# Splitting and shifting the token preparation inside a sixteen-head attention loop

## The reference

```python
def _layer_norm(x, scale, offset):
    mu = jnp.mean(x, axis=-1, keepdims=True)
    var = jnp.var(x, axis=-1, keepdims=True)
    return (x - mu) * jax.lax.rsqrt(var + LN_EPS) * scale + offset
...
h = _layer_norm(x, ln1_scale, ln1_offset)
x = res + _cross_attention(h, xf_1, ...)      # 16 heads: q from h, k and v from the context
h = _layer_norm(x, ln2_scale, ln2_offset)
x = res + _cross_attention(h, xf_2, ...)
h = _layer_norm(x, ln_mlp_scale, ln_mlp_offset)
h = gelu(h @ w_fc1 + b_fc1) @ w_fc2 + b_fc2
return x + h
```

## Time and profile before

| | before |
|---|---|
| median of 3 runs | 1243.47 us (1241.01 to 1245.72) |
| profiled execution: its time | 1242.29 us |
| profiled execution: its span | 1240.8 us |
| busy, PE / DVE / ACT / POOL | 1198.8 / 888.7 / 779.0 / 598.1 us |
| mean granted TensorE clock | 0.995 |

### The profile page before, as it was taken

How to read it: one execution, slowest core, us unless ns; L and a number is a source line. 1 busy time by engine, 2 the same in 40 slices (tenths; PEclk the granted TensorE clock), 3 DMA queues, 4 the chain that set the end, 5 groups by cost and what they waited for, 6 DMA issues and landing times.

```text
span 1240.8 us, 27130 instructions
## 1 busy us (share of the span) xinstructions
PE 1198.8 (97%) x9933; PEld 1027.3 (83%) x9933; DVE 888.7 (72%) x2304; ACT 779.0 (63%) x1889; POOL 598.1 (48%) x966
## 2 busy tenths in 40 slices
PE   9999999999999999999989899999999899999997
PEld 8999999999999999999978565786675587666664
DVE  6887868778887787778864788536788564667764
ACT  5876666668866666566774566746776643555553
POOL 4874645558865454555852443504444131324333
PEclk9999999999999999999999999999999999999999
DMA  6541001104430001001320220122322012221100
GB/s 193 157 123 32 27 26 33 34 27 123 142 94 27 26 28 34 27 27 35 123 70 27 81 81 29 52 73 71 88 64 70 20 54 61 59 65 44 39 11 19
DMA packets 56820, 75.03 MB, mean 60 GB/s; under 512 B 11312, under 2 KB 30576, under 8 KB 56688
## 3 DMA queue, kind: packets, MB, share of 16 engines
q1 hardware_dynamic: 51568, 72.75, 19.5%
q0 software_dynamic: 5120, 0.56, 0.3%
HBM read 49.46 MB, written 1.05 MB: 41 GB/s over the span
## 4 chain that ended last, share of the span: by engine, by line
PE 81%; DVE 7%; issue 5%; ACT 4%; POOL 2%; DMA 1%; ACTq 0%; DVEq 0%; POOLq 0%
PE bank L125 19%; PE bank L127 18%; PE bank L126 18%; PE bank L2053 5%; PE bank L771 4%; PE bank L2000 3%; PE bank L2010 3%; PE bank L1986 2%; PE bank L2011 2%; ACT PT L2127 2%; PE bank L1982 2%; PE bank L178 1%; DMA Q<-rows 1%; PE bank L713 1%; PE bank L1737 1%
## 5 line engine op out<-in xcount | busy, mean ns | idle before, releaser
L1095 POOL TENSOR_SCALAR E<-E,rl 128x256 f32<-128x256 f32 x256 | 243.8, 963 | 213.6 <-DVE rl L980 213.4
L2127 ACT ACTIVATE PT<-bank 128x512 f32<-128x512 f32 x320 | 173.4, 594 | 92.2 <-PE bank L2011 56.0
L846 ACT ACTIVATE QTh<-bank,bqs 128x256 fp32r<-128x256 f32 x128 | 60.7, 474 | 151.4 <-PE bank L127 151.3
L2208 DVE CUSTOM_DVE_ANT_0 Em<-bank,M 128x256 bf16<-128x256 f32 x256 | 95.1, 420 | 53.7 <-PE bank L1986 22.3
L856 ACT ACTIVATE E<-bank,nm 128x257 f32<-128x257 f32 x256 | 119.4, 480 | 1.2 <-DVE nm L950 1.1
L984 DVE TENSOR_TENSOR PTl<-bank,PTh 128x512 fp32r<-128x512 f32 x128 | 88.0, 688 | 27.6 <-ACT PTh L868 27.1
L957 DVE SCALAR_TENSOR_TENSOR QTl<-bank,bqs,QTh 128x256 fp32r<-128x256 f32 x128 | 61.6, 481 | 63.0 <-ACT KT L847 62.2
L868 ACT CAST PTh<-bank 128x512 fp32r<-128x512 f32 x128 | 75.2, 587 | 43.7 <-PE bank L771 43.6
L2202 DVE TENSOR_REDUCE nm<-bank 128x1 f32<-128x512 f32 x128 | 83.4, 686 | 22.1 <-PE bank L1982 21.4
L950 DVE TENSOR_REDUCE nm<-bank 128x1 f32<-128x257 f32 x256 | 95.4, 415 | 0.0
L2000 PE MATMUL bank<-Q,K 51*128 51x256 f32 (+1 forms) x640 | 85.5, 315 | 4.4 <-DMA Q<-rows 1.9
(11 more groups left out here) (438 smaller groups left out, 4374.5 us busy)
## 6 DMA issues: line engine op xcount, KB each, us to landing
stage<-in_wts SPq DMA_DIRECT2D x99, 256.0 KB, 3.3
U<-in_vrows SPq DMA_DIRECT2D x64, 256.0 KB, 2.7
K<-stage SPq DMA_DIRECT2D x48, 128.0 KB
Q<-stage SPq DMA_DIRECT2D x48, 128.0 KB
K<-stage SPq DMA_DIRECT2D x48, 64.0 KB
Q<-stage SPq DMA_DIRECT2D x48, 64.0 KB
K<-xh SPq DMA_DIRECT2D x16, 128.0 KB, 3.0
Q<-rows POOLq DMA_DIRECT2D x96, 4.0 KB, 1.8
```

The lines of the kernel that those rows point to most:

```text
L1095: m = pool.tensor_scalar(s.E[:, i % 3, t, 0:256], s.E[:, i % 3, t, 0:256], s.rl[:, r, t:t + 1], None, ALU.mult)
L2127: act.activation(s.PT[i % s.NPT][:, 2 * u:2 * u + 2, :].rearrange("p a b -> p (a b)"), s.STB[y][:], ACT.Exp).then_inc(S["t_ex"])
L2208: dve.tensor_tensor_reduce(out=s.Em[:, (2 * i + e) % 4], in0=bank[:, e * 256:e * 256 + 256], in1=s.M3[:, j, e, :], scale=-1.0, scalar=3.4e ...
```

## The change

Counted modulo 16, for the seven seams:

| step | engine | pass before | pass after |
|---|---|---|---|
| statistics | VectorE | 7, both tiles and the aggregation | 6 and 7, one tile each; aggregation in 8 |
| root | GpSimd | 7 | 8 |
| normalisation | VectorE | 8, both tiles | 9 and 10, one each |
| `turn_x` | TensorE | 9 | 11 |
| scaling | VectorE | 10, both halves | 12 and 13, one each |
| `tokens_high`, `tokens_low` | ScalarE, VectorE | 11 | 14 |

The first MLP batch's steps move from passes 114, 115, 116, 118 to 111, 112, 113, 114 and 116; the second one's statistics from 119 to 118 and its scaling from 121 to 122. The number of operations and their sizes stay as they are.

```diff
-AHEAD = {114: [(0, "stats")], 115: [(0, "norm")], 116: [(0, "turn"), (0, "scale")], 118: [(0, "parts")],
-         119: [(1, "stats")], 120: [(1, "norm")], 121: [(1, "turn"), (1, "scale")], 127: [(1, "parts")]}
+AHEAD = {111: [(0, "stats")], 112: [(0, "norm")], 113: [(0, "turn")], 114: [(0, "scale")], 116: [(0, "parts")],
+         118: [(1, "stats")], 120: [(1, "norm")], 121: [(1, "turn")], 122: [(1, "scale")], 127: [(1, "parts")]}
...
-        if t % 16 == 9 and t // 16 < 7:
+        if t % 16 == 11 and t // 16 < 7:
             turn_x(t // 16 + 1)
...
-        if t % 16 == 11 and t // 16 < 7:
+        if t % 16 == 14 and t // 16 < 7:
             tokens_high(t // 16 + 1)
...
+    def half_stats(n, t):
+        w.wait_ge(S[f"ld_x{n}"] if n < 4 else S["dve_x"], 16 if n < 4 else n - 3)
+        z = dve.bn_stats(s.scr["st"][:, t, :], batch_x(n)[:, t, :])
...
+    def half_norm(n, t):
+        w.wait_ge(S["dve_hlo"], n)
+        w.wait_ge(S["ln_rsqrt"], n + 1)
...
-            if t % 16 == 7:
-                stats(n)
+            if t % 16 in (6, 7):
+                half_stats(n, t % 16 - 6)
             if t % 16 == 8:
-                norm(n)
-            if t % 16 == 10:
-                scaled(n)
-            if t % 16 == 11:
+                moments(n)
+            if t % 16 in (9, 10):
+                half_norm(n, t % 16 - 9)
+            if t % 16 in (12, 13):
+                half_scaled(n, t % 16 - 12)
+            if t % 16 == 14:
                 tokens_low(n)
...
-            if t % 16 == 7:
+            if t % 16 == 8:
                 rsqrt(t // 16 + 1)
```

More of the change, by code:

```diff
@@ L925, in stats, with moments @@
         ln_stats(dve, w, S, "ln", n, batch_x(n), s.scr)
+    def half_stats(n, t):
+        w.wait_ge(S[f"ld_x{n}"] if n < 4 else S["dve_x"], 16 if n < 4 else n - 3)
+        z = dve.bn_stats(s.scr["st"][:, t, :], batch_x(n)[:, t, :])
+        if t == 1:
+            z.then_inc(S["ln_stats"])
+    def moments(n):
+        w.wait_ge(S["ln_stats"], n + 1)
+        dve.bn_aggr(s.scr["mv"][:, 0, :], s.scr["st"][:, 0, :])
+        dve.bn_aggr(s.scr["mv"][:, 1, :], s.scr["st"][:, 1, :]).then_inc(S["ln_moments"])
+    def half_norm(n, t):
+        w.wait_ge(S["dve_hlo"], n)
+        w.wait_ge(S["ln_rsqrt"], n + 1)
+        z = dve.tensor_scalar(xn[:, t, :], batch_x(n)[:, t, :], s.scr["mv"][:, t, 0:1], s.scr["rs"][:, 4 + t:5 + t],
+                              ALU.subtract, ALU.mult)
+        if t == 1:
+            z.then_inc(S["ln_xn"])
     def norm(n):
@@ L929, in norm, with half_scaled @@
         ln_norm(dve, w, S, "ln", n, batch_x(n), s.scr)
+    def half_scaled(n, d):
+        a = n // 4
+        w.wait_ge(S["pe_hT"], n + 1)
+        w.wait_ge(S["ld_cols"], 16)
+        z = dve.tensor_scalar(xn[:, d, :], s.MISC[:, d * 256:d * 256 + 256], c.col("ln_s", a, d), c.col("ln_o", a, d),
+                              ALU.mult, ALU.add)
+        if d == 1:
+            z.then_inc(S["dve_hf"])
     def scaled(n):
```

## The result

The changed kernel takes 1254.1 us, the median of 6 runs (1250.56 to 1255.09), against 1243.49 for the kernel before: a ratio of 1.0079, 95% interval 1.0067 to 1.0092, thus 8 to 11 us slower. Its profiled execution took 1253.96 us, its span is 1252.5.

What follows compares the result with a forecast made beforehand. TensorE, busy 97% of the span, bounds the kernel. Waits +10.9, port +1.0, gains -4.0 make +7.9 us: 1250.2 from the profiled 1242.29, put at 1250.8 as halfway to the median's offset; range 1246.5 to 1256.

Steps and rivals of the forecast that it cites:

- The sign and its cause: Slower, chance 0.76: in heads 15 modulo 16 TensorE waits for `hTl`, which runs behind `PTl`; sum +7.9 us.
- the port lost everywhere: Rival, chance 0.12: GpSimd wins the shared port at all seven seams, 3.6 us in place of 1.0; about 1253.4.
- the gains absent: Rival, chance 0.08: the removed waits return behind another operation, only 1 us gained; +10.9, about 1254.
- The wait's size: TensorE's wait for `hTl` at each seam: 1.44 us standing still, 1.55 with refill, 10.9 for seven.
- The port: VectorE and GpSimd contend for a port at `hTl`; two of seven seams lost, 2 x 0.52 = 1.0 us.
- The trace agrees on who blocks whom: Claim that the trace fits the skill's first-comer lock rule, though head 41 shows 0.52 us, not the rule's 0.78.
- The clock: Rival, chance 0.03: standing still halves TensorE's clock for a head, another 4.7 us per seam, +33 in all.
- The gains: Waits removed: five seams 1.4, seam 1 0.75, seam 4 0.85, MLP batches 1.0; together 4.0 us.
- the 0.2 that was to come back in heads 58 and 62: Seam 4: heads 56 and 60 lose their waits, 0.2 us returns in heads 58 and 62; net -0.85.
- The MLP's part: First and second MLP batch, heads 112, 116 and 120: moving their steps forward saves 1.0 us.
- hidden by one whole head: GpSimd's root, moved one pass, costs nothing: the normalisation needing it comes two half steps later, covered by 4.72 us.
- The forecast's own range: +5.5 to +10.5 us, chance 0.62, from the port's bounds and gains between 2.5 and 5.4.

Runs made afterwards that it cites:

- e1: The changed kernel with both token steps still in pass 14, but ahead of `heads_out` and `probs` on ScalarE and VectorE: 1241.79 us.
- e2: The kernel before with only the two token steps moved from pass 11 to pass 14, nothing split: 1253.99 us.
- e6: The kernel of e1 with the two token steps back in their late place in pass 14 at the first seam alone: 1243.47 us.
- e8: The changed kernel with two more unread tile statistics on VectorE ahead of each `hTl` of the loop, 0.34 us each: 1257.52 us.
- e4: The changed kernel with GpSimd's root moved from the end of pass 8 to pass 9, behind the key column: 1250.62 us.
- e3: The kernel before with only the new `AHEAD` table for the MLP's first tokens: 1242.86 us, ratio 1.0000.
- e10: The kernel before, nothing split: statistics and root moved to pass 6, token steps to pass 12, plus the MLP's new table: 1239.47 us.

## Why the prediction came out as it did

**The sign and its cause were right.** 1254.1 lies within 1246.5 to 1256, and the mechanism is shown both ways: e1 takes the wait away and leaves the splitting, e2 leaves the splitting out and makes the wait. The number alone would not show this: two of the rivals, at 1253.4 (the port lost everywhere) and 1254 (the gains absent), lie nearer to 1254.1 than the forecast's 1250.8. The heads rule them out: `hTl` took 1.22 at one seam of seven, and the waits in heads 24, 40, 72, 88, 104 and 116 are gone.

**The wait's size, 1.55 a seam: right.** Five heads show 6.25 or 6.26, against 4.72 undisturbed. 10.9 was reckoned for seven; e2's loop, where the hTl-wait of head 12 and half of head 60's went at the same time, grew by 10.0.

**The port: two lost seams were assumed, one was.** In head 15 `U` came first:

```profile
87.13 1.22 DVE L971 TENSOR_TENSOR hTl<-xn,hTh 128x512 fp32r<-128x512 f32 x1
...
87.08 0.72 POOL L1119 TENSOR_TENSOR U<-U 128x256 f32<-128x256 f32 x1
```

`hTl` took 1.22 in place of 0.68, 0.54 more against the 0.52 assumed. In head 63 it took 0.84 while GpSimd's scaling of `E` ran, and the head took 6.45 in place of 6.25. Together 0.7 us, for a term of 1.0. The Trainium skill's rule ("SBUF — State Buffer", Who interferes with whom) has the right loser here: `U` started 0.05 earlier and kept its length. But `hTl` would then have started only at the end of `U`, 87.80, and ended at 88.48; it ended at 88.35. And the prediction's "The trace agrees on who blocks whom" doesn't hold for head 41: by the earlier trace rows the normalisation started 0.03 before `U` there, and paid all the same. Recorded starts so close together don't settle who comes first.

**The clock: given a chance of 0.03, and it happened, once.** Head 15 took 8.33. With the wait and the port alone it takes 6.80 (e6), so the clock cost 1.5 us. That is far less than the 4.7 a seam of the rival: it was low for a part of the head, and at one seam of seven. The window below, inside head 15 of the changed kernel, shows the lower of the two levels, 1.2 GHz:

```profile
89.40:92.70 3.30, 3.30 (x17) 0.50 0.03 7
```

TensorE stood still until 88.41, and its matmuls grow from 0.28 to 0.41 us from 89.35 on. It is not the length of the standing still by itself that decides, by e6 and e8. What does is open; the same place fell in two executions of three (changed kernel and e4, not e6), and I can't say more than that.

**The gains: 4.0 reckoned, 4.4 came.** The seven seam heads are 3.62 (head 15) + 1.74 (head 63) + 5 x 1.54 = 13.1 us longer, head 57 another 0.94; the loop as a whole is 9.57 longer, so the other heads gained 4.4 (9.57 - 13.1 - 0.94). Seam 1's heads 8, 10 and 14 read 5.07, 5.15 and 5.19, thus 0.35, 0.43 and 0.45 over, with a half step beside a weight piece (reckoned: 0.30, 0.30, 0.41), and head 12 is free. Heads 56 and 60 lost their waits, and the 0.2 that was to come back in heads 58 and 62 didn't. The MLP's part gave 1.3 for 1.0 (e3).

**The step that failed is the root.** The prediction had it "hidden by one whole head". That looked only at who waits for the root's result. The price was paid by what stands behind it on GpSimd, the key column of the next head, and only at seam 4, where the first weight pieces had by then made GpSimd late: 0.94 us in head 57 (e4).

**The sum again.** Measured in the loop: 10.8 for the waits, 0.7 for the port, 1.5 for the clock, 0.9 for the root, less 4.4 of gains, +9.5. Reckoned: 10.9, 1.0, 0 and 0, less 4.0, +7.9. The two terms that were put at nothing, 2.4 us together, are partly offset by 0.7 us of misses in the others, which is luck. Another 2.1 us of the profiled execution lie outside the loop. The forecast's own range has a slip: with its bounds, the port at 3.6 and the gains at 2.5, the top is +12.0 and not +10.5; 1254.1 lies inside either way.

## What to carry to other kernels

Where an engine is busy 97% of the time, read who waits for the end of a moved chain before counting what the chain's parts no longer disturb: spreading a chain pushes its end later, and the last step here met its reader. The pass in which a step is written isn't the time at which it runs; what stands in front of it in its queue decides, and e1 regained 11 us in the loop by moving the token steps ahead of two others in the same pass. Before splitting work into smaller parts, look for a stretch where the whole part has nothing critical behind it: e10, in the one execution traced, has the shortest loop with no part split. And for every step that is moved, price what is queued behind it, not only what depends on it.

## What the hardware showed beyond that

A standing still of 1.80 us by the profile was followed by a fall of TensorE's clock (from 2.4 to 1.2 GHz for a part of the head, mean 0.80) in two executions, and by none in a third; seven of 1.92 to 1.97 us in e8 were followed by none. The program up to head 15 is nearly the same in the three. An experiment that shows such a fall once doesn't price it.
